# Inverse roots moved from ScalarE to VectorE, two loads moved later, and the queries' stacking DMAs issued by GpSimd, in a four-block transformer kernel

## The chip, the core and the metric

The kernel runs on one core of one Trainium2 chip. The core has five instruction streams: TensorE (PE, with its weight loads shown as PEld), VectorE (DVE), ScalarE (ACT), GpSimd (POOL) and SyncE (SP). They meet only at semaphores. The metric is the device time of one execution in microseconds (us). Batches, groups and units are counted from 0.

## The reference

For 8 batches of 512 tokens with 512 features the reference computes four residual blocks:

```python
x = x + attention(layernorm(x), ctx, ctx, Wq, bq, Wk, bk, Wv, bv, Wo, bo)   # 16 heads of 32
x = x + routed_experts(layernorm(x), Wc, bc, W1, b1, W2, b2)                # 32 experts, 4 sets, 32 wide
x = x + mlstm_heads(layernorm(x), ctx, ctx, igate, fgate)                   # 8 heads of 64, gated decay, RMS norm per head
x = x + bitlinear_ffn(layernorm(x), W1, b1, W2, b2)                         # 512 -> 2048 -> 512, 8-bit tokens, ternary weights

layernorm(x) = (x - mean) / sqrt(var + 1e-5)
rms(h)       = h * rsqrt(mean(h * h) + 1e-6)
```

All inputs and outputs are float32.

## The kernel before

Three phases follow each other, each a block of its own with the streams written out by hand: attention (`attention_phase`, names a_), experts (`experts_phase`, names b_) and the tail (`tail_phase`, names c_), which does the third and fourth block together. The experts' phase is not changed.

**Attention.** A batch has 64 units, one for each pair of a head and a tile of 128 queries. 16 units (4 heads by 4 tiles) form a group, so that a batch has the groups 0 to 3. The loop variable g runs over all units and some steps beyond the last; u is its place in the batch. In step g, PE does the score matmul of unit g+2 (`scores`, L604), the four transposes of the probabilities of unit g-1 (L612), every fourth step the mix with the values (L630), and one share of a product (K, Q, V, O or the router's L, after the list PRODUCTS; L680). DVE takes the maximum of a score tile (L491), ACT the exponential (L424), and the two take turns in copying the transposed probabilities out (L317).

The score matmul reads `stack["Q"]` and `stack["K"]`, in which each head's 32 rows stand four times, as high and low halves in two orders. The product of queries or keys for a group is split by ACT (high half, L415) and DVE (low half, `low`, L485) into `parts`; then 16 DMAs of 64 KB within SBUF (`stack_parts`, L309) write them into one of two stacks. The issuing queue first waits until the last score of the group two before has been done, and for DVE's low half. Before ACT writes `parts` for the next group, it waits until all 16 DMAs of the last one of the same kind have landed (`wait_stack` in `product_out`). ACT is in order: while it waits there, no exponential is made.

SP issues the 16 DMAs for the keys and then the 16 for the queries of a group (all but the first group's queries, which ACT issues), and in between the stores of the results. In each batch after the first, the splits fall in these steps: keys 1 in u=0, queries 1 in u=4, keys 2 in u=8, queries 2 in u=12, keys 3 in u=24, queries 3 in u=28; and keys 0 and queries 0 of the next batch in u=44 and 48. ACT issues the load of the next batch's x (`a_xs`) in u=4, of the residual x (`a_x`, L463) of the batch before in u=6, and of the context in u=33. POOL adds the output bias to the residual x, four adds (L368), and does nothing else.

The layernorm (class `Norm`) is spread over DVE's steps: statistics (L145), moments (L151), scale (L158), result (L162). In between, ACT takes the square root (`on_scalar`, L177). Its function is in another table than the exponential, so that ACT loads a table before and after it.

**Tail.** A Fori loop runs over the batches. Turn m does the mLSTM heads of batch m and the feed-forward block of batch m-1; at its end DVE runs one chain: moments and scale of the next batch's layernorm (`normalize_x2`), the heads' normalizer and RMS scale (L1597 to L1608), the products (L1610, L1618), the layernorm before the feed-forward (`on_vector`), and the 8-bit rounding of the tokens (L1623 to L1631, `c_xq`). PE begins the next turn with transposes of `c_xq` (L1651). There are three square roots on ACT in a turn.

Of the kernel before, what the change touches and what calls it, by code (L numbers as in the profile page):

```python
# [6 lines left out]
F32R = mybir.dt.float32r  # L7
ALU = mybir.AluOpType
# [3 lines left out]
P = 128  # L12
B, S, D = 8, 512, 512
T = S // P
# [115 lines left out]

class Norm:
# [3 lines left out]
    def __init__(self, ctx, sems, nc, name):  # L135
        self.nc = nc
        sb = lambda n, shape: ctx.enter_context(nc.sbuf_tensor(f"{name}_{n}", shape, F32))
        self.stats, self.mv, self.rstd = sb("stats", [P, T, 6]), sb("mv", [P, T, 2]), sb("rstd", [P, T])
        self.std = sb("std", [P, T])
        self.eps = sb("eps", [P, 1])  # L140
        self.var_ready = sems.make(f"{name}_var_ready")
        self.std_ready = sems.make(f"{name}_std_ready")
# [4 lines left out]
    def moments(self, dve, chain, last):  # L147
# [5 lines left out]
        dve.sem_inc(self.var_ready, 1)  # L153

    def scale(self, dve, chain, b):

        dve.wait_ge(self.std_ready, b + 1)
        chain.step(self.nc.vector.reciprocal(self.rstd[:, :], self.std[:, :]))  # L158
# [6 lines left out]
    def on_vector(self, dve, chain, b, src, dst):  # L165
# [4 lines left out]
        self.scale(dve, chain, b)  # L170
# [3 lines left out]

    def on_scalar(self, act, b):
        act.wait_ge(self.var_ready, b + 1)
        self.nc.scalar.activation(self.std[:, :], self.mv[:, :, 1], ACT.Sqrt,  # L177
                                  bias=self.eps[:, 0:1]).then_inc(self.std_ready, 1)


def attention_phase(nc, sems, A, scratch):
# [39 lines left out]
    STATS_AT, SCALE_AT, RESULT_AT = 14, 20, 21  # L221
# [25 lines left out]
    with ctx:  # L247
# [44 lines left out]
        filled, tie_ready, wq_ready, bo_ready, bo_full = (sem(n) for n in ("filled", "tie_ready", "wq_ready", "bo_ready", "bo_full"))  # L292
        sp_parted, pe_parted, act_parted = sem("sp_parted"), sem("pe_parted"), sem("act_parted")
        STACKED = 16 * 4 * HM
        N_LOADS = 6
# [16 lines left out]
        with nc.Block() as block:  # L312
# [8 lines left out]
            def _(sp):  # L321
                sp.dma_start(cs[:, :, :], tiled(A["ctx_1024"])[0]).then_inc(c_in, 16)
                sp.dma_start(w["Wk"][:, :, :], A["L0_xattn_Wk"].rearrange("(c p) n -> p c n", p=P)).then_inc(w_in["Wk"], 16)
                for name in ("Wv", "Wo"):
                    sp.dma_start(w[name][:, :, :], A["L0_xattn_" + name].rearrange("(c p) n -> p c n", p=P)).then_inc(w_in[name], 16)
# [30 lines left out]
            def _(pool):  # L356
                for ring in (work, score, turn, mix):
                    ring.give_ahead(pool)
                for norm in (norm0, norm1):
                    nc.gpsimd.memset(norm.eps[:, :], LN_EPS).then_inc(filled, 1)  # L360
# [3 lines left out]
                pool.wait_ge(bo_ready, 1)  # L364
                for b in range(B):
                    pool.wait_ge(x1_in, b * 16 + 16)
                    for t in range(T):
                        last = nc.gpsimd.tensor_tensor(x1[:, t, :], x1[:, t, :], bo[:, :], ALU.add)  # L368
                    last.then_inc(res_ready, 1)

            @block.scalar
            def _(act):
                act.dma_start(xs[:, :, :], tiled(A["x"])[0]).then_inc(x_in, 16)
                act.dma_start(w["Wq"][:, :, :], A["L0_xattn_Wq"].rearrange("(c p) n -> p c n", p=P)).then_inc(w_in["Wq"], 16)
                for name, tile in (("bq", bq), ("bk", bk), ("bv", bv)):
                    act.dma_start(tile[:, :], A["L0_xattn_" + name].rearrange("(c p) -> p c", p=P),
                                  allow_slow_non_contiguous=True).then_inc(loaded, 16)
# [3 lines left out]
                act.wait_ge(filled, 2)  # L381
# [47 lines left out]
                norm0.on_scalar(act, 0)  # L429
                act.wait_ge(loaded, 16 * N_LOADS)  # L430
                nc.scalar.mul(bq[:, :], bq[:, :], SCALE).then_inc(wq_ready, 1)
                act.wait_ge(w_in["Wq"], 16)
                nc.scalar.mul(w["Wq"][:, :, :], w["Wq"][:, :, :], SCALE).then_inc(wq_ready, 1)
# [5 lines left out]
                stack_parts(act, "Q", 0)  # L439
                act.dma_start(cs[:, :, :], tiled(A["ctx_1024"])[1]).then_inc(c_in, 16)  # L440
                for t in range(T):
                    product_out("V", 0, t)

                for g in range(STEPS):
# [10 lines left out]
                    if u == 4 and b + 1 < B:  # L455
                        act.wait_ge(xs_read, b + 1)
                        act.dma_start(xs[:, :, :], tiled(A["x"])[b + 1]).then_inc(x_in, 16)
                    if u == 6 and 1 <= b <= B:
                        if b >= 2:
                            act.wait_ge(x1_stored, (b - 1) * 16)  # L460
                            act.wait_ge(xn1_ready, b - 1)
# [4 lines left out]
                    if u == 33 and b + 2 < B:  # L466
                        act.dma_start(cs[:, :, :], tiled(A["ctx_1024"])[b + 2]).then_inc(c_in, 16)
                    if u == 39 and b >= 1:
                        norm1.on_scalar(act, b - 1)
# [5 lines left out]
            def _(dve):  # L475
# [59 lines left out]
                norm0.on_vector(dve, chain, 0, xs, xn).then_inc(xn_ready, 1)  # L535
# [4 lines left out]
                dve.wait_ge(bo_full, 1)  # L540
# [1290 lines left out]
```

## Time and profile before

| | us |
|---|---|
| median of 3 runs (2638.3 to 2654.33) | 2644.69 |
| the profiled execution, its own time | 2646.36 |
| its span, first to last instruction | 2644.6 |
| PE busy | 2224.4 (84%) |
| DVE busy | 1459.3 (55%) |
| ACT busy | 1411.9 (53%) |
| POOL busy | 365.0 (14%) |
| mean granted clock of TensorE | 0.906 |

The attention phase takes about the first 1190 us, the experts' phase the time to about 1580, the tail the rest. A busy share is the time in which an engine executes, over the span. In the timeline, the number in square brackets is the idle time of the engine ahead of a row, and behind the arrow stands what ended it. "SPq" and "ACTq" rows are DMA issues; their duration is that of the issue and not of the transfer.

### The profile page before, as it was taken

What the parts mean: (1) busy time and instruction counts of PE and PEld (TensorE: products, weight loads), DVE (VectorE), ACT (ScalarE), POOL (GpSimd) and SP (SyncE); (2) the same over time, 40 slices, a digit from 0 to 9 for tenths busy, and PEclk for the clock granted to TensorE, in tenths of its full rate; (3) what the DMA queues carried; (4) which work ended last, traced back from release to release, by engine and by line L of the source; (5) the groups of instructions that cost most, each with busy time, mean ns of one, the idle gap of its engine ahead of it and who ended that gap; (6) DMA issues with size and microseconds to landing.
All of it is one profiled execution on the core that took longest, in us unless ns stands there. A gap on an engine that the chain in (4) does not pass through costs nothing. (4 is left out here: it accounts for less than half of the span.)

```text
span 2644.6 us, 43219 instructions
## 1 busy us (share of the span) xinstructions
PE 2224.4 (84%) x14571; PEld 1402.8 (53%) x14571; DVE 1459.3 (55%) x2518; ACT 1411.9 (53%) x3038; POOL 365.0 (14%) x513
## 2 busy tenths in 40 slices
PE   6899999999999999876888854969888897979765
PEld 2565656565656565546647521646445454646442
DVE  1656566666665565642332322576766757566754
ACT  2665656565656565631332423766566574656553
POOL 0000000000000000002112100331313132231310
PEclk9999999999999999988998986779797888979787
DMA  4324343343333333316666667522212132132100
GB/s 151 97 77 116 87 104 112 97 120 97 112 97 105 94 91 87 96 56 167 176 229 175 192 220 249 196 96 69 87 59 93 57 121 89 62 99 68 34 15 16
DMA packets 200656, 288.78 MB, mean 109 GB/s; under 512 B 29408, under 2 KB 91904, under 8 KB 195264
## 3 DMA queue, kind: packets, MB, share of 16 engines
q1 hardware_dynamic: 157664, 232.86, 29.3%
q10 hardware_dynamic: 42848, 54.02, 6.8%
q8 instruction: 88, 1.44, 0.2%
q14 instruction: 56, 0.46, 0.1%
HBM read 156.62 MB, written 63.05 MB: 83 GB/s over the span
## 5 line engine op out<-in xcount | busy, mean ns | idle before, releaser
L491 DVE TENSOR_REDUCE a_negmax<-a_score 128x1 f32<-128x512 f32 x512 | 345.6, 684 | 120.4 <-PE a_score L604 110.5
L604 PE MATMUL a_score<-a_k_stack,a_q_stack 128*128 128x512 f32 x512 | 354.2, 692 | 67.4 <-ACT a_prob L424 67.4
L424 ACT ACTIVATE a_prob<-a_score,a_negmax 128x512 f32<-128x512 f32 x512 | 353.9, 694 | 57.0 <-DVE a_negmax L491 56.8
L612 PEld LDWEIGHTS a_turn<-a_ident,a_prob 128*128 128x128 f32 x2048 | 256.2, 142 | 132.3 <-issue 91.2
L317 ACT COPY a_probT<-a_turn 128x512 f32<-128x512 f32 x256 | 150.0, 586 | 325.4 <-PE a_turn L612 324.3
L612 PE MATMUL a_turn<-a_ident,a_prob 128*128 128x128 f32 x2048 | 311.9, 275 | 3.1 <-ACT a_perm L400 2.0
L317 DVE COPY a_probT<-a_turn 128x512 f32<-128x512 f32 x256 | 176.7, 690 | 244.4 <-PE a_turn L612 243.5
L1237 POOL TENSOR_SCALAR c_diag<-c_negm,c_aL 128x128 f32<-128x128 f32 x256 | 165.6, 664 | 342.7 <-issue 119.4
L1705 PE MATMUL c_work<-c_xT,c_cT 64*128 64x512 f32 (+3 forms) x512 | 179.2, 496 | 39.7 <-DVE c_decay L1473 39.7
L368 POOL TENSOR_TENSOR a_x<-a_x,a_bo 128x512 f32<-128x512 f32 x32 | 39.6, 1269 | 1122.5 <-DMA a_x<-in_x 1122.5
L604 PEld LDWEIGHTS a_score<-a_k_stack,a_q_stack 128*128 128x128 f32 x512 | 98.5, 192 | 175.3 <-ACT a_prob L424 89.0
L1705 PEld LDWEIGHTS c_work<-c_xT,c_cT 64*128 64x128 f32 x512 | 102.5, 210 | 136.0 <-issue 72.8
L1718 PE MATMUL c_mix<-c_v,c_decay 128*128 128x65 f32 x1280 | 174.0, 297 | 0.0
L1718 PEld LDWEIGHTS c_mix<-c_v,c_decay 128*128 128x128 f32 x1280 | 167.9, 212 | 4.7 <-issue 0.7
L1473 DVE SCALAR_TENSOR_TENSOR c_decay<-c_work,c_decay 128x512 f32<-128x512 f32 (+3 forms) x256 | 109.9, 483 | 91.2 <-PE c_work L1705 70.5
L869 PE MATMUL b_work<-b_blocks,b_xn 128*128 128x256 f32 x512 | 128.0, 415 | 26.3 <-POOL b_blocks L841 23.4
L1731 PE MATMUL c_ff<-c_w1T,c_xqT 128*128 128x512 bf16 x512 | 136.9, 429 | 11.3 <-ACT c_xqT L1262 11.3
L630 PE MATMUL a_mix<-a_probT,a_v 128*32 128x128 f32 x4096 | 145.7, 285 | 0.1
L1747 PE MATMUL c_ff<-c_w2T,c_hqT 128*128 128x512 bf16 x512 | 135.3, 424 | 10.6 <-ACT c_hqT L1278 10.6
L905 PE MATMUL b_work<-b_w2T,b_inner 128*128 128x512 f32 x256 | 126.5, 642 | 21.1 <-ACT b_inner L954 21.1
L1286 ACT ACTIVATE c_decay<-c_negm,c_aL 128x384 f32<-128x384 f32 (+2 forms) x192 | 83.5, 498 | 109.3 <-PE c_mix L1718 90.7
L869 PEld LDWEIGHTS b_work<-b_blocks,b_xn 128*128 128x128 f32 x512 | 123.4, 329 | 31.3 <-issue 24.1
(189 smaller groups left out, 3704.3 us busy)
## 6 DMA issues: line engine op xcount, KB each, us to landing
a_k_stack<-a_k_parts SPq DMA_DIRECT2D x512, 64.0 KB, 2.0
scratch_res<-b_res SPq DMA_DIRECT2D x32, 1024.0 KB, 4.7
c_res<-scratch_res SPq DMA_DIRECT2D x32, 1024.0 KB, 9.5
a_q_stack<-a_q_parts SPq DMA_DIRECT2D x496, 64.0 KB, 2.0
b_xn<-scratch_xn SPq DMA_DIRECT2D x68, 256.0 KB, 2.7
c_hid<-in_L_ffn_W ACTq DMA_DIRECT2D x16, 1024.0 KB, 5.2
c_negm<-scratch_m SPq DMA_DIRECT2D x64, 256.0 KB, 3.6
a_xs<-in_x ACTq DMA_DIRECT2D x8, 1024.0 KB, 6.8
```

What stands on the lines that cost most here:

```text
L317: copy(probT[:, U // HM % 2, U % HM, :, :], turn.bank(entries["P", U])[:, :].rearrange("p (k q) -> p k q", k=T)).then_inc(turn.free[entrie ...
L424: nc.scalar.activation(prob[:, U % 4, :], score.bank(U)[:, :], ACT.Exp, bias=negmax[:, u:u + 1], accum_out=sums[:, head_of(U), tile_of(U): ...
L491: nc.vector.tensor_reduce(negmax[:, U % UNITS:U % UNITS + 1], score.bank(U)[:, :], AX.X, ALU.max, negate=True).then_inc(max_ready, 1)
L604: nc.tensor.matmul(score.bank(U)[:, :], stack["Q"][:, M % 2, g, t * P:(t + 1) * P], stack["K"][:, M % 2, g, :], start=True, stop=True).the ...
L612: last = nc.tensor.transpose(turn.bank(j)[:, k * P:(k + 1) * P], prob[:, U % 4, k * P:(k + 1) * P], ident[:, :])
L630: last = nc.tensor.matmul(mix.bank(M)[g * DH0:(g + 1) * DH0, cols], v[:, b % 2, k, h * DH0:(h + 1) * DH0], probT[:, q % 2, g, k, :], start ...
L869: last = nc.tensor.matmul(work.bank(j)[:, c * EH * GT:(c + 1) * EH * GT], xc[:, 2 * half + c, :], blocks[:, t].rearrange("p e g -> p (e g) ...
L1237: last = nc.gpsimd.tensor_scalar(diag[:, h % 2, t, :], negm[:, h % 4, t * P:(t + 1) * P], aL[:, 0, t, h:h + 1], None, ALU.add)
L1705: last = nc.tensor.matmul(work.bank(j)[:, i0:i0 + S - t * P], cT[r, h // 2, t * P:(t + 1) * P], xT[r, h // 2, t * P:S], start=True, stop=True)
L1718: last = nc.tensor.matmul(mix.bank(job)[:, i * (DH1 + 1):(i + 1) * (DH1 + 1)], row_of(h, j, i * P, (i + 1) * P), head_of(v, h)[:, j], star ...
L1731: last = nc.tensor.matmul(ff.bank(j)[:, :], xqT[:, c, t * P:(t + 1) * P], w1T[:, c, k * 512:(k + 1) * 512], start=c == 0, stop=c == C - 1)
L1747: last = nc.tensor.matmul(ff.bank(j)[:, :], hqT[:, k, :], w2T[:, k, :], start=k == 0, stop=k == HC - 1)
```

## The change

- The square roots go. `inverse_root` computes 1/sqrt(value + eps) on DVE in 12 chained small steps: an integer shift and subtraction give a first guess, three Newton rounds of three steps refine it. Each step waits for the one before. It replaces ACT's root and DVE's reciprocal in all layernorms and in the RMS scale. In the attention loop its four parts stand in u=17 to 20 for the next batch's layernorm (statistics now in u=13 to 16), and in u=37 and 38 for the one before the experts.
- The load of x for the batch after the next is issued in u=26, the residual x in u=44 of its own batch, the context in u=43.
- SP issues the keys' stacking DMAs only. The queries' come from POOL's queue: groups 1, 2 and 3, then the wait for the residual x and the four adds, then group 0 of the next batch.
- At the start, Wk and Wq are loaded in two parts, the first 128 columns ahead; the last V product, the second K product and the bias product (L698) come after the first two scores, and the bias product inside the loop.

```diff
+def inverse_root(nc, step, dst, src, eps, value, square, parts=range(4)):
+    if 0 in parts:
+        step(nc.vector.tensor_scalar(value, src, eps, None, ALU.add))
+        step(nc.vector.tensor_scalar(dst.bitcast(I32), value.bitcast(I32), 1, None, ALU.logical_shift_right))
+        step(nc.vector.tensor_scalar(dst.bitcast(I32), dst.bitcast(I32), -1, 0x5F3759DF, ALU.mult, ALU.add))
+    for _ in [k for k in parts if k > 0]:
+        step(nc.vector.tensor_tensor(square, dst, dst, ALU.mult))
+        step(nc.vector.scalar_tensor_tensor(square, square, -0.5, value, ALU.mult, ALU.mult))
+        step(nc.vector.scalar_tensor_tensor(dst, square, 1.5, dst, ALU.add, ALU.mult))
...
 # SP
-                    stack_parts(sp, "Q", b * GROUPS + 1)
                     for m in (2, 3):
-                        for kind in ("K", "Q"):
-                            stack_parts(sp, kind, b * GROUPS + m)
+                        stack_parts(sp, "K", b * GROUPS + m)
...
                     if b + 1 < B:
-                        for kind in ("K", "Q"):
-                            stack_parts(sp, kind, (b + 1) * GROUPS)
+                        stack_parts(sp, "K", (b + 1) * GROUPS)
 # POOL
-                pool.wait_ge(bo_ready, 1)
+                stack_parts(pool, "Q", 0)
                 for b in range(B):
+                    for m in (1, 2, 3):
+                        stack_parts(pool, "Q", b * GROUPS + m)
+                    pool.wait_ge(bo_ready, 1)
                     pool.wait_ge(x1_in, b * 16 + 16)
                     for t in range(T):
                         last = nc.gpsimd.tensor_tensor(x1[:, t, :], x1[:, t, :], bo[:, :], ALU.add)
                     last.then_inc(res_ready, 1)
+                    if b + 1 < B:
+                        stack_parts(pool, "Q", (b + 1) * GROUPS)
 # ACT, in the loop over g
-                    if u == 4 and b + 1 < B:
-                        act.dma_start(xs[:, :, :], tiled(A["x"])[b + 1]).then_inc(x_in, 16)
-                    if u == 6 and 1 <= b <= B:
-                        act.dma_start(x1[:, :, :], tiled(A["x"])[b - 1]).then_inc(x1_in, 16)
-                    if u == STATS_AT + T + 1 and b + 1 < B:
-                        norm0.on_scalar(act, b + 1)
-                    if u == 39 and b >= 1:
-                        norm1.on_scalar(act, b - 1)
+                    if u == 26 and b + 2 < B:
+                        act.dma_start(xs[:, :, :], tiled(A["x"])[b + 2]).then_inc(x_in, 16)
+                    if u == 44 and b < B:
+                        act.dma_start(x1[:, :, :], tiled(A["x"])[b]).then_inc(x1_in, 16)
 # DVE, tail
-                    dve.wait_ge(rms_ready, m + 1)
-                    step(nc.vector.reciprocal(f3[:, :, :], f2[:, :, :]))
+                    inverse_root(nc, step, f3[:, :, :], f2[:, :, :], 1e-6, f4[:, :, :], f5[:, :, :])
```

## Rows read from the trace of the kernel before

**Rows 1.** Busy time in a stretch: length, then PE, PEld, DVE, ACT, POOL, clock, DMA.
```profile
204.00:344.00 140.00, 131.64 (x1041) 84.28 (x1040) 86.37 (x150) 84.36 (x195) 4.94 (x4) 0.99 0.38 103
```
**Rows 2.** Waits from 60 to 1153 us: total, times, longest.
```profile
PE a_score L604 <- ACT a_prob L424: 67.4, 30, 4.8
...
ACT a_k_parts L415 <- DMA a_k_stack<-a_k_parts: 35.2, 8, 6.0
ACT a_q_parts L415 <- DMA a_q_stack<-a_q_parts: 6.4, 2, 3.8
```
**Rows 3.** Timeline around the stall of batch 2: start, duration, engine, line, operation.
```profile
330.25 10.01 SPq L309 DMA_DIRECT2D a_k_stack<-a_k_parts  x16
337.17 0.74 DVE L485 SCALAR_TENSOR_TENSOR a_q_parts<-a_work,a_bq,a_q_parts 128x512 fp32r<-128x512 f32 x1
337.40 0.38 ACTq L463 DMA_DIRECT2D a_x<-in_x  x1
340.36 10.63 SPq L309 DMA_DIRECT2D a_q_stack<-a_q_parts  x16
347.36 0.69 ACT L415 ACTIVATE a_k_parts<-a_work,a_bk 128x512 fp32r<-128x512 f32 x1 [4.92 <-DMA a_k_stack<-a_k_parts]
348.76 0.67 PE L604 MATMUL a_score<-a_k_stack,a_q_stack 128*128 128x512 f32 x1 [3.71 <-ACT a_prob L424]
350.21 1.93 PE L630 MATMUL a_mix<-a_probT,a_v 128*32 128x128 f32 x32
355.19 0.69 ACT L415 ACTIVATE a_q_parts<-a_work,a_bq 128x512 fp32r<-128x512 f32 x1
```
**Rows 4.** Busy time just behind that stall; the clock is the last but two.
```profile
350.00:352.00 2.00, 2.00 (x34) 1.36 (x32) 1.29 (x2) 0.54 (x2) 2.00 (x2) 0.50 0.42 110
```
**Rows 5.** Lines of ACT, 60 to 1150 us: busy, mean ns, idle.
```profile
L177 ACT ACT_TABLE_LOAD x14 | 18.0, 1283 | 0.3
```
**Rows 6.** Timeline: PE behind a square root in batches 0, 1 and 7.
```profile
107.26 0.50 PE L604 MATMUL a_score<-a_k_stack,a_q_stack 128*128 128x512 f32 x1 [2.38 <-ACT a_prob L424]
...
276.24 0.50 PE L604 MATMUL a_score<-a_k_stack,a_q_stack 128*128 128x512 f32 x1 [1.55 <-ACT a_prob L424]
...
1112.66 0.50 PE L604 MATMUL a_score<-a_k_stack,a_q_stack 128*128 128x512 f32 x1 [3.71 <-ACT a_prob L424]
```
**Rows 7.** Line L309, issues: ns least, median, most; and time to landing.
```profile
L309 SPq DMA_DIRECT2D a_k_stack<-a_k_parts x512: 507/591/2077, 27.8 to 1097.7; - x171
...
DMA to landing us min/median/max: 1.9/2.0/8.7
```
**Rows 8.** Timeline: ACT's stacking issues at the start.
```profile
34.74 10.57 ACTq L309 DMA_DIRECT2D a_q_stack<-a_q_parts  x16
```
**Rows 9.** Line L604: ns least, median, most; first and last start.
```profile
L604 PE MATMUL a_score<-a_k_stack,a_q_stack x512: 398/795/1240, 63.8 to 1148.5; 128*128 128x512 f32 x171
```
**Rows 10.** Timeline at the end of the attention phase.
```profile
1165.20 7.13 PE L680 MATMUL a_work<-a_Wo,a_attnT 128*128 128x512 f32 x16 [2.00 <-DVE a_x L516]
```
**Rows 11.** Timeline of one tail turn's chain on DVE, and PE behind it.
```profile
2080.33 0.38 DVE L151 BATCH_NORM_AGGREGATE c_norm_mv<-c_norm_stats 128x2 f32<-128x6 f32 x4 [0.33 <-DVEq L104]
2081.43 1.91 DVE L162 TENSOR_SCALAR c_xn<-c_x,c_norm_mv,c_norm_rstd 128x512 f32<-128x512 f32 x4
...
2084.75 0.19 DVE L1605 TENSOR_TENSOR c_f<-c_f 128x32 f32<-128x32 f32 x1
...
2085.72 0.19 DVE L1608 TENSOR_TENSOR c_f<-c_f 128x32 f32<-128x32 f32 x1
...
2104.91 1.89 PE L1651 MATMUL c_ff<-c_identb,c_xq 128*128 128x128 bf16 x16 [6.61 <-DVE c_xq L1631]
```
**Rows 12.** Timeline of the same turn: small DVE steps beside POOL's adds.
```profile
2096.98 4.93 POOL L1248 TENSOR_TENSOR c_x<-c_x,c_b 128x512 f32<-128x512 f32 x4 [40.30 <-DVEq L1622]
...
2099.53 0.18 DVE L1625 RECIPROCAL c_xr<-c_xscale 128x4 f32<-128x4 f32 x1
2099.74 0.97 DVE L1626 TENSOR_SCALAR c_xr<-c_xr 128x4 f32<-128x4 f32 x1
```

More of the change, by code:

```diff
@@ L7 @@
 F32R = mybir.dt.float32r
+I32 = mybir.dt.int32
 ALU = mybir.AluOpType
@@ L152, in moments, with scale @@
         chain.step(last, apart=True)
[L153 to L158, printed above, removed]
+    def scale(self, chain, parts=range(4)):
+        inverse_root(self.nc, chain.step, self.rstd[:, :], self.mv[:, :, 1], LN_EPS, self.value[:, :], self.square[:, :], parts)
     def tile_result(self, src, dst, t):
@@ L163, in tile_result, with on_vector @@
                                             ALU.subtract, ALU.mult)
-    def on_vector(self, dve, chain, b, src, dst):
+    def on_vector(self, dve, chain, src, dst):
         for t in range(T):
@@ L169, in on_vector @@
         self.moments(dve, chain, last)
-        self.scale(dve, chain, b)
+        self.scale(chain)
         for t in range(T):
@@ L173, in on_vector @@
         return last
[L175 to L178, printed above, removed]
 def attention_phase(nc, sems, A, scratch):
@@ L534, in _ @@
                 dve.wait_ge(x_in, 16)
-                norm0.on_vector(dve, chain, 0, xs, xn).then_inc(xn_ready, 1)
+                norm0.on_vector(dve, chain, xs, xn).then_inc(xn_ready, 1)
                 dve.wait_ge(xn_ready, 1)
@@ L539, in _ @@
                 low("Q", 0, 0)
-                dve.wait_ge(bo_full, 1)
-                nc.vector.tensor_tensor(bo[:, :], bo[:, :], mix.bank(0)[:, :], ALU.add).then_inc(bo_ready, 1)
                 maximum(0)
@@ L553, in _ @@
                                 low(*job)
+                    if g == 3:
+                        dve.wait_ge(bo_full, 1)
+                        nc.vector.tensor_tensor(bo[:, :], bo[:, :], mix.bank(0)[:, :], ALU.add).then_inc(bo_ready, 1)
                     if g % UG == 0 and UG <= g <= ALL:
@@ L570, in _ @@
                             norm0.moments(dve, chain, last)
-                        if u == SCALE_AT:
-                            norm0.scale(dve, chain, b + 1)
+                        if SCALE_AT <= u < SCALE_AT + 4:
+                            norm0.scale(chain, (u - SCALE_AT,))
                         if RESULT_AT <= u < RESULT_AT + T:
@@ L579, in _ @@
                     if b >= 1:
+                        if u in (37, 38):
+                            norm1.scale(chain, (2 * (u - 37), 2 * (u - 37) + 1))
                         if u == 39:
-                            norm1.scale(dve, chain, b - 1)
                             if b >= 2:
@@ L692, in _ @@
                 pe.wait_ge(w_in["Wv"], 16)
-                for t in range(T):
+                for t in range(T - 1):
                     product("V", 0, t, range(C))
-                pe.wait_ge(w_in["Wo"], 16)
-                pe.wait_ge(loaded, 16 * N_LOADS)
-                for c in range(C):
-                    last = nc.tensor.matmul(mix.bank(0)[:, :], bv[:, c:c + 1].to_broadcast([P, P]), w["Wo"][:, c, :],
-                                            start=c == 0, stop=c == C - 1)
-                last.then_inc(bo_full, 1)
-                pe.wait_ge(bo_ready, 1)
-                product("K", 0, 1, range(C))
                 for U in range(AHEAD):
                     scores(U)
+                product("V", 0, T - 1, range(C))
+                pe.wait_ge(w_in["Wk"], 16)
+                product("K", 0, 1, range(C))
+                pe.wait_ge(wq_ready, 3)
                 for g in range(STEPS):
@@ L717, in _ @@
                         turn_tiles(*job)
+                    if g == 1:
+                        pe.wait_ge(w_in["Wo"], 16)
+                        pe.wait_ge(loaded, 16 * N_LOADS)
+                        pe.sem_inc(pe_parted, 1)
+                        for c in range(C):
+                            last = nc.tensor.matmul(mix.bank(0)[:, :], bv[:, c:c + 1].to_broadcast([P, P]), w["Wo"][:, c, :],
+                                                    start=c == 0, stop=c == C - 1)
+                        last.then_inc(bo_full, 1)
 def experts_phase(nc, sems, A, scratch):
@@ L1037, in tail_phase @@
         b1, b2 = sb("b1", [P, HID]), sb("b2", [P, D])
-        one, eps6 = sb("one", [P, 1]), sb("eps6", [P, 1])
+        one = sb("one", [P, 1])
         rnd = sb("rnd", [P, 1])
@@ L1055, in tail_phase @@
         hraw = sb("hraw", [P, T, PAIRS, 2 * DH1 + 2])
-        f1, f2, f3 = (sb(f"f{k}", [P, T, H1]) for k in range(3))
+        f1, f2, f3, f4, f5 = (sb(f"f{k}", [P, T, H1]) for k in range(5))
         square, sumsq = sb("square", [P, T, DH1]), sb("sumsq", [P, T, H1])
@@ L1404, in turn @@
                                 load_weight(PIECES + h + 1)
-                        if next_too and h == H1:
-                            norm0.on_scalar(act, m + 1)
-                    if m is not None:
-                        act.wait_ge(meansq_ready, m + 1)
-                        nc.scalar.activation(f2[:, :, :], f2[:, :, :], ACT.Sqrt, bias=eps6[:, :]).then_inc(rms_ready, 1)
                     if next_too:
@@ L1509, in normalize_x2 @@
                     norm0.moments(dve, chain, last)
-                    norm0.scale(dve, chain, m)
+                    norm0.scale(chain)
                     for t in range(T):
@@ L1619, in turn @@
                     step(last)
-                    step(norm1.on_vector(dve, chain, m, x3, x2))
+                    step(norm1.on_vector(dve, chain, x3, x2))
                     dve.sem_inc(x3_read, 1)
```

80 lines of the change are left out of this document (40 added, 40 removed).

## Prediction

> **What bounds the kernel now.** I read the busy time by stage first. In a full batch of the attention phase PE is busy 131.64 of 140 us and DVE and ACT about 86 each [rows 1]: PE sets the pace, and only its gaps of some 8 us a batch can be won there. The list of waits says what the gaps are: nearly all of them, 67.4 us, are score matmuls that wait for an exponential [rows 2]. ACT's own waits show the cause of over half: 35.2 us for the keys' stacking DMAs and 6.4 us for the queries', in ten waits [rows 2]. The timeline shows one. ACT comes to the split of keys 2 at 347.36 - 4.92 = 342.44 us, the DMAs of keys 1 were issued from 330.25 to 340.26, and yet they land 5 us late, behind a 1 MB load issued at 337.40 (and one of the same size two units ahead of it); PE idles 3.71 us of the 4.92 [rows 3]. Behind it the granted clock is 0.50, that is 1.2 GHz instead of 2.4 [rows 4], and a mix takes 1.93 us [rows 3]; with some 2.9 us at half clock such a stall costs 1.4 us more. The rest of the gaps stands behind table loads: 14 loads of the root's table at 1.28 us [rows 5], each followed by one back to the exponential's, with PE idle 2.38 us behind the next batch's layernorm, 1.55 us behind the other, and 3.71 us in batch 7, where no products fill the steps [rows 6].
>
> The tail is bound otherwise. At a turn's end PE waits 6.61 us for `c_xq`, the last link of DVE's chain [rows 11]. What makes that chain longer makes the turn longer.
>
> **The change part by part.** All of it is set against the profiled execution, 2646.36 us with a span of 2644.6; the median of the runs is 1.7 us below it.
>
> *Loads moved.* With x issued in u=26, the residual in u=44 and the context in u=43, no 1 MB load runs beside the stacking of keys 1. SP ends its issues at 340.26, and with 2.0 us from an issue to its landing [rows 7] the last lands at about 341.6, ahead of ACT's 342.44 [rows 3]. The ten waits go, if nothing takes their place. PE loses about 1.2 us less than ACT in each (3.71 against 4.92), so 41.6 - 9 x 1.2 = 31 us. Seven of them are about as long as the one shown, and I give them its lower clock too: 7 x 1.4 = 10 us. Together -41. The moved loads collide with the stacking of keys 0 and queries 0 of the next batch, which is needed some 16 units later: nothing.
>
> *Roots in the attention loop.* ACT loses both loads and the root. PE gets back 7 x 2.38 + 6 x 1.55 + 3.71 and 1.4 for the clock in batch 7 [rows 6]: -31. DVE gets 12 steps for each. A small step starts 0.21 us after the last one (2099.53 to 2099.74) [rows 12]. DVE idles (140 - 86.37) / 64 = 0.84 us in a unit [rows 1], so three steps (0.63) in each of u=17 to 20 fit, and six (1.26) in u=37 and 38 are 0.4 too many each: 7 x 0.8, and a little more in batch 7, whose units are short: +7 (0 to 15).
>
> *The queries' DMAs on POOL.* SP issues less, which frees nothing that PE waits for once the loads have gone, except that queries 1 no longer wait for SP to end keys 1 (340.36 against DVE's end at 337.91) [rows 3]. What counts is when they land. ACT needs all 16 to be down when it comes to the split of queries 2. In the run before it comes there 7.83 us after that of keys 2 (347.36 to 355.19), 1.4 of it due to the low clock [rows 3]; without the stall it comes at 342.44 + 6.4 = 348.8, which is 10.9 us after DVE's low half of queries 1. If POOL needs r us for an issue, the last lands 16 r + 1.4 us after it, 1.4 being the landing's 2.0 less one issue. ACT waits 16 r - 9.5, and PE 1.2 us less; where PE's stall is as long as the one shown, 1.4 for the clock comes on top. Behind ACT's wait stand the exponentials, and so PE. The trace has no DMA issued by POOL. The nearest rows are the same 16 transfers on SP (10.01 / 16 = 0.63 us each) and on ACT (10.57 / 16 = 0.66) [rows 3, 8]; a single one takes up to 2.08 [rows 7]. Below it is bounded by 0.51, the shortest issue. I take r = 1.0: nearer to the many than to the one, but above them, since both rows are of the other two queues and it would be chance if POOL's way of making a transfer cost the same. Then ACT waits 6.5 us, PE 5.3 + 1.4 = 6.7, in eight batches +53 us; +52, since queries 1 of batch 0 have a little more room. At r = 0.63 it is 0.6 us, within the slack, and nothing; at 1.3, 11.3 - 1.2 + 1.4 = 11.5 us or +92; at 2.08 POOL would issue for 133 us of a batch and set its pace, beyond +180. The other groups have room at r = 1.0: queries 2, 3 and 0 take 18 us and have 15 units or more, about 31 us, except group 0, which stands behind the residual's load and adds and has about 23.
>
> The Trainium skill (DMA: Bandwidth & Descriptors, "Latency and other measured facts") gives about 1 us to the first byte for a DMA issued by GpSimd and 0.6 us for one from the other queues. If the difference of 0.4 lies in each issue, r is 0.63 + 0.4 = 1.03, and the sum is mine; if it lies only once in the way of each transfer, r stays 0.63 and the sum is the first rival's. No row of this trace says which.
>
> *The start.* ACT no longer issues 16 DMAs (34.74 to 45.31) [rows 8], so the V copies are made at once; the first score, now at 63.8 [rows 9], goes ahead of two products but waits for POOL's 16: 34.74 + 16 + 1.4 = 52 us. Two scores, two products (3.5 us each) and the bias product in the loop follow, and the two added load issues of 0.5 us each stand ahead of ACT's first copy: +2 (-4 at r = 0.63, +7 at 1.3).
>
> *The last batch.* Its residual is there early, which saves the 2.00 us of PE's wait [rows 10]; its last root is on the path and costs 1.8 more. Nothing.
>
> *Roots in the tail.* A layernorm's scale takes 2081.43 - 2080.71 = 0.72 us from the end of the moments to the first result [rows 11], since ACT has loaded its table ahead. Twelve steps at 0.21 are 2.52: +1.80. The RMS root takes 2085.72 - 2084.75 = 0.97 us with the step ahead of it [rows 11]; after, 13 x 0.22 = 2.86: +1.89. A turn gets +5.5, all in the chain that PE waits 6.61 us for; PE's own transposes in between are later by 1.8 only, and are hidden. Eight turns: +44; I take +41, since the first turn has its root behind other work of ACT's (36 to 48). What ACT saves in the tail hides behind the same wait.
>
> Sum: -41 - 31 + 7 + 52 + 2 + 41 = +30 on 2646.4: **2676 us**.
>
> **The rivals.**
>
> *POOL issues as fast as SP.* For it: the transfers are the same 64 KB, and the small POOL instructions are not slow. Against it: no row has such an issue. Then the +52 goes, and the start gives 4 where it took 2, rounded to -3: -41 - 31 + 7 - 3 + 41 = -27, 2619 us. This is the case on the other side. It decides between r = 0.75 and 0.85: at 0.85 ACT waits 4.1 us and PE 2.9, 23 us over eight batches, and the sum is near nothing.
>
> *POOL issues at 1.3 us or more.* Then +92 stands for +52, the start costs 6 or 7, and queries 0 (16 x 1.3 + 1.4 = 22 us behind the adds, against some 23) begin to hold up the next batch's scores, about 1 us each, +8: -72 + 7 + 92 + 7 + 8 + 41 = +83, about 2728 us.
>
> *The added steps on DVE are slowed by POOL.* Such a thing has a row: beside POOL's four adds a 128x4 tensor_scalar takes 0.97 us where the reciprocal ahead of it takes 0.18 [rows 12]. If POOL's making of descriptors acts as its adds do, the three such steps of u=17, which now stand beside the issues for queries 2, cost 2.4 us more, less the slack 0.8: 7 x 1.6 = +11, 2687 us. The Trainium skill (SBUF — State Buffer, "Who interferes with whom") says that DVE's two-port modes and GpSimd lock each other out, and that descriptors made by GpSimd wait for such an operation. The trace agrees for the adds, by the 0.97; for descriptors nothing here shows it.
>
> **How the numbers follow.** I give 0.37 to the forecast (r of 0.85 to 1.15, own range 2646 to 2702), 0.33 to the first rival, 0.25 to the second, 0.05 to the third alone. The range of 8 in 10 goes from just under the first rival to just over the second: 2614 to 2734. This kernel's runs can tell a change of about 0.5%, 13 us. Slower by more than that come out the second and third rivals (0.29 of 0.30) and most of the forecast's case (0.28 of 0.37): 0.57. Faster is the first rival but for its upper edge, and a sliver of the others: 0.30. The same: 0.13.
>
> **What would show it.** A POOL queue row `a_q_stack` with 16 issues in about 16 us; ACT's waits for the keys' DMAs gone and one of about 6 us a batch for the queries' in u=12; no root tables on ACT; DVE's time from the moments to `c_xn` at 2.5 us in place of 0.72, and PE's wait for `c_xq` near 10 us with the turn 5.5 us longer. The forecast is wrong if POOL's 16 issues take 12 us or less, or over 20, or if the root's step isn't near 0.21 us.

## The result, and the profile after

The changed kernel takes 2615.56 us (median of 4 runs, 2610.33 to 2623.96) against 2645.79 us for the kernel before beside it: a ratio of 0.9893, interval 0.9866 to 0.9919. The forecast was 2676 us and slower; the kernel is 30 us faster. The profiled execution took 2620.14 us with a span of 2618.4.

By stages of the profiled executions (attention ends where PE starts `b_aux`, the tail starts with PE's first `c_mix`):

| stage | before | after | difference |
|---|---|---|---|
| start and attention phase | 1199.39 | 1115.32 | -84.1 |
| experts phase (same code) | 390.2 | 385.3 | -4.9 |
| tail | 1055.0 | 1117.8 | +62.8 |

The attention phase brought more than forecast and the tail cost more. The experts' code is the same in every kernel here and took 384 to 396 us in the profiled executions, so its -4.9 says nothing. First the page of the changed kernel: the busy times, the queues, and time from issue to landing.

```profile
PE 2216.2 (85%) x14571; PEld 1398.9 (53%) x14571; DVE 1524.9 (58%) x2958; ACT 1347.6 (51%) x2952; POOL 616.1 (24%) x1020
...
q0 software_dynamic: 16384, 33.59, 5.0%
q8 instruction: 88, 1.44, 0.2%
q14 instruction: 89, 0.73, 0.1%
...
a_k_stack<-a_k_parts SPq DMA_DIRECT2D x512, 64.0 KB, 2.7
a_q_stack<-a_q_parts POOLq DMA_DIRECT2D x512, 64.0 KB, 2.3
```

The answer to [rows 1] is the busy time of a stretch of 128 us in batches 2 and 3. A middle batch, from its first score to the next batch's, now takes 130.7 us where it took 139.5 to 143. PE idles 0.8 us of the stretch, and its clock is full (1.00, that is 2.4 GHz).

```profile
322.00:450.00 128.00, 127.23 (x1026) 81.38 (x1025) 88.17 (x170) 78.14 (x187) 36.17 (x68) 1.00 0.39 112
```

The answer to [rows 2], the waits of the attention phase (total, times, longest): PE's 67.4 us behind exponentials are 7.6, ACT's 35.2 and 6.4 us for stacks are 4.0 and 0.7.

```profile
PE a_score L614 <- ACT a_prob L434: 7.6, 10, 2.3
ACT a_k_parts L425 <- DMA a_k_stack<-a_k_parts: 4.0, 7, 0.7
ACT a_q_parts L425 <- DMA a_q_stack<-a_q_parts: 0.7, 1, 0.7
```

The row that the forecast hung on, from the timeline of POOL (start, duration): 16 issues in 7.81 us, that is 0.49 us each, where SP took 0.63 [rows 3]. The third rival, that POOL's issues slow DVE's added steps, falls with the same trace: the 128x4 steps of the roots take 0.16 to 0.18 us in the attention phase, as long as in the run below that has the roots on DVE and no issue on POOL.

```profile
324.79 7.81 POOL L316 DMA_DIRECT2D a_q_stack<-a_q_parts  x16 [6.25 <-DVE a_q_parts L493]
```

In the tail the answers to [rows 11] are a timeline of one turn on DVE and PE. From the last aggregate to the layernorm's first result it is now 2.71 us (2161.29 to 2164.00). PE waits 10.86 us for `c_xq`, 4.3 more than before. Two rows have no forerunner: DVE starts the next turn 3.19 us after its last instruction, "issue" being the cause, and PE then waits 2.49 us for the hidden layer.

```profile
2160.91 0.38 DVE L164 BATCH_NORM_AGGREGATE c_norm_mv<-c_norm_stats 128x2 f32<-128x6 f32 x4 [0.15 <-DVEq L105]
2161.44 0.17 DVE L138 TENSOR_SCALAR c_norm_value<-c_norm_mv 128x4 f32<-128x4 f32 x1 [0.15 <-DVEq L105]
...
2164.00 1.92 DVE L173 TENSOR_SCALAR c_x<-c_x,c_norm_mv,c_norm_rstd 128x512 f32<-128x512 f32 x4 [0.21 <-DVE c_norm_rstd L144]
...
2174.05 1.89 PE L1657 MATMUL c_ff<-c_identb,c_xq 128*128 128x128 bf16 x16 [10.86 <-DVE c_xq L1637]
2177.11 0.74 DVE L1531 TENSOR_SCALAR c_gate_rows<-c_work,c_gb 8x512 f32<-8x512 f32 x1 [3.19 <-issue]
...
2183.82 1.89 PE L1737 MATMUL c_ff<-c_w1T,c_xqT 128*128 128x512 bf16 x4 [2.49 <-DVE c_hid L1438]
```

In the kernel before the same instruction came 0.70 us after `c_xq`:

```profile
2105.47 0.74 DVE L1524 TENSOR_SCALAR c_gate_rows<-c_work,c_gb 8x512 f32<-8x512 f32 x1 [0.70 <-DVE c_xq L1631]
```

The stall stands at the head of the five turns that DVE's loop jumps back to (3.19 to 3.54 us). The turn that enters the loop and the one behind it have 0.42 and 0.39. And the DMA view of one turn of the changed kernel (1918.4 to 2048 us) has a line that no middle turn of the kernel before has, instruction packets (their number, MB, share):

```profile
q14 instruction: 5, 0.04, 0.1%
```

### The profile page after: what moved, and what is told of

Its sections match the earlier page's. It is cut to its first block and busy times, and to the rows that moved or that the text cites. A ratio compares the mean times of both kernels' runs of the same rounds, so it can differ in the third digit from the quotient of the medians.

```text
span 2618.4 us, 43758 instructions
## 1 busy us (share of the span) xinstructions
PE 2216.2 (85%) x14571; PEld 1398.9 (53%) x14571; DVE 1524.9 (58%) x2958; ACT 1347.6 (51%) x2952; POOL 616.1 (24%) x1020
## 5 line engine op out<-in xcount | busy, mean ns | idle before, releaser
L316 POOL DMA_DIRECT2D a_q_stack<-a_q_parts x512 | 250.8, 498 | 513.1 <-DVE a_q_parts L493 253.8
L1711 PE MATMUL c_work<-c_xT,c_cT 64*128 64x512 f32 (+3 forms) x512 | 185.2, 510 | 39.7 <-DVE c_decay L1480 39.7
L1737 PE MATMUL c_ff<-c_w1T,c_xqT 128*128 128x512 bf16 x512 | 142.3, 439 | 18.7 <-ACT c_xqT L1278 10.5
L643 PE MATMUL a_mix<-a_probT,a_v 128*32 128x128 f32 x4096 | 138.4, 276 | 0.1
```

The source lines that it names most:

```text
L316: eng.dma_start(stack[kind][i * DH0:(i + 1) * DH0, M % 2, g, :].bitcast(F32), parts[kind][g * DH0:(g + 1) * DH0, part, :].bitcast(F32)).th ...
L1711: last = nc.tensor.matmul(work.bank(j)[:, i0:i0 + S - t * P], cT[r, h // 2, t * P:(t + 1) * P], xT[r, h // 2, t * P:S], start=True, stop=True)
L1737: last = nc.tensor.matmul(ff.bank(j)[:, :], xqT[:, c, t * P:(t + 1) * P], w1T[:, c, k * 512:(k + 1) * 512], start=c == 0, stop=c == C - 1)
```

## The experiments

Two theories were at stake. In the attention phase: POOL's queue costs nothing at 0.49 us an issue, and the loads, the queries' queue and the roots each bring a part; which part brings what was open. In the tail: the roots' chain is only half the loss, and the other half is DVE's loop, whose longer code is fetched again in every turn. The kernel before was measured again beside each of three groups of the twelve kernels; its medians were 2644.47, 2647.38 and 2649.64 us, and a difference of some 5 us between groups is scatter.

**The tail's roots back on ACT** (the faster kernel of the two halves)

```
 tail_phase: as in the kernel before (ACT Sqrt, reciprocal on DVE); attention_phase: as changed
```

> The changed kernel with the tail's three roots a turn back on ACT, as before (attention phase and start as changed). Theory: the tail lost 63 us (1055.0 to 1117.8 from the first mix on PE to the end) through its roots on DVE and nothing else, so this kernel takes 2616 - 63 = 2553 us, with a turn back at 119.5 us and DVE starting a turn 0.7 us after c_xq. Rival 1: part of the loss came from outside (the clock's history or other phases): then only the 44 us of my own chain price come back, 2572 us. Rival 2: the attention phase's gain of 84 us depends on nothing in the tail; if it shrank here, the phases would not add up and the time would be above 2580.

2564.64 us, ratio 0.9692 (0.9653 to 0.973). The tail is back at 1056.7 us, the turns are 119.4 us, DVE starts them after 0.70. So the whole of the tail's loss is undone, which the first rival denied, and the attention phase's gain stays (1116.77), which the second did. The total is 12 us above the theory's figure: 61 us went from the tail, but the profiled run of the changed kernel, from whose 62.8 the figure was made, was 4.6 us above its median, and the experts phase took 3.4 us more here.

**Only the tail's roots on DVE**

```
 tail_phase: as changed; attention_phase: as in the kernel before
```

> The mirror image: the kernel before with only the tail's roots moved to DVE. Theory: before + 63 = 2708 us, turns of 126 to 130 us, DVE starting a turn of the loop over 3 us after c_xq with instruction packets in each turn. Rival: the price in my prediction, +41 to +44, 2687 to 2690 us.

2723.65 us, ratio 1.029 (1.025 to 1.033): +79, more than either. The tail takes 1137.4 us, 82 more than before. The same loop body, yet DVE's stall is 5.3 to 5.6 us, and the hidden layer waits 4.8:

```profile
2157.86 0.74 DVE L1570 TENSOR_SCALAR c_gate_rows<-c_work,c_gb 8x512 f32<-8x512 f32 x1 [5.52 <-issue]
...
2164.58 1.89 PE L1776 MATMUL c_ff<-c_w1T,c_xqT 128*128 128x512 bf16 x4 [4.81 <-DVE c_hid L1477]
```

So the stall depends on more than the body. The code ahead of the loop differs; whether the loop's place among the fetched blocks decides was not tried.

**The changed kernel with DVE's turns written out**

```
+            if eng is nc.vector:
+                for b in range(B - 2):
+                    turn(b + 1, b, True)
+            else:
                 with eng.Fori(0, B - 2) as b:
                     turn(b + 1, b, True)
```

> The changed kernel with DVE's six middle turns of the tail written out instead of in a loop (the other engines keep theirs). Theory: DVE's loop body of 345 instructions in the built program (282 before) no longer fits what the engine holds, so that each turn of the loop starts with a stall of 3.2 us and instruction packets; written out, the instructions come ahead of need, the stall of five turns goes and with it the later hidden layer and its low clock: 5 turns of 129.5 become 125 us or less, 2616 - 22 = 2594 us or lower. Rival 1: the stall is the branch itself or the wait for another engine's loop: the same 3.2 us stay, 2616. Rival 2: the added turn length is the longer chain alone and the stall is hidden: the stall goes but the time falls under 5 us.

2594.57 us, ratio 0.9799 (0.9769 to 0.9829): 21 us off, as the theory said (in the profiled executions the tail alone is 32 us shorter, 1085.7 for 1117.8, so the loop's price is 20 to 30 us). In place of the stall stand 0.23 us:

```profile
2164.34 0.74 DVE L1535 TENSOR_SCALAR c_gate_rows<-c_work,c_gb 8x512 f32<-8x512 f32 x1 [0.23 <-DVE c_xq L1641]
```

Both rivals fall. The turns are 123.0 to 124.8 us for the first run's 119.4, so the chain alone costs some 4 us a turn.

**The first run with 64 increments in DVE's loop**

```
                         if m is not None and h < H1:
                             head_product(m, h)
+                        if 1 <= h:
+                            for _ in range(8):
+                                dve.sem_inc(dve_parted, 1)
```

> The kernel of the first run (roots of the tail on ACT, DVE's loop body 282 instructions, no stall at its start) with 64 semaphore increments added to DVE's loop of the tail, eight behind each head's product, where DVE has time; they bring its body to 346 instructions and lengthen no chain of data. Theory: the stall at the loop's start is a matter of the number of instructions, so it appears here at 3 to 5.5 us in five turns with instruction packets in each, and the turn grows by 2 to 5 us: 2565 + 10 to 25 = 2580 us. Rival: the stall needs the root's instructions (their register operations or the chain); then none appears and the time stays at 2565, or gains a few us by the increments' own time.

2586.63 us, ratio 0.9768 (0.9741 to 0.9795): 22 us above the first run. No root is on DVE's path here, and the stall and its packets (five in the turn from 2034 us on) appear, first the timeline, then the DMA view:

```profile
2159.93 0.74 DVE L1591 TENSOR_SCALAR c_gate_rows<-c_work,c_gb 8x512 f32<-8x512 f32 x1 [3.19 <-issue]
```

```profile
q14 instruction: 5, 0.04, 0.1%
```

The turns that end in the stall are 121.1 to 123.4 us long, where the first run has 118.6 to 119.5. The one turn of the loop without a stall at its end is 120.1 for 119.2, so the increments' own time is 1 us at most. With the run before it, this shows that a loop longer by 63 or 64 instructions brings the stall, whatever they compute. That count alone sets it is not shown: the run with only the tail's roots on DVE has the same count and a longer stall.

**The first run with DVE's turns written out** (the edit of the last run but one)

> The kernel of the first run (2565 us) with DVE's six middle turns of the tail written out. Its loop has no stall, only 0.70 us between c_xq and the next turn's first instruction, which becomes 0.23. Theory: nothing to win but that: 5 x 0.5 = 2.5 us, 2562. Rival: the register instructions that prepare a loop's wait values (81 of 282) cost time on the chain to c_xq, and the written-out form, which waits on constants, brings 10 us or more, 2555; the run of the changed kernel written out had turns of 123.3 us where the chain's price in the prediction, 5.5, would have given 125.

2561.49 us, ratio 0.9655 (0.962 to 0.969), 3 us below the first run, which is within the scatter. The rival falls: in the changed kernel a 128x4 step of a root starts 0.20 us after the last in the loop and 0.20 written out, so the register instructions cost nothing there. Against the changed kernel written out, this one gives the chain's price alone: 2594.57 - 2561.49 = 33 us by the medians. The tail's stage says less, 1085.7 - 1062.2 = 24 us against this run and 29 against the first, so the chain costs about 30.

**Queries back on SP** (otherwise the first run)

```
                         stack_parts(sp, "K", b * GROUPS + 1)
-                    for m in (2, 3):
-                        stack_parts(sp, "K", b * GROUPS + m)
+                    stack_parts(sp, "Q", b * GROUPS + 1)
+                    for m in (2, 3):
+                        for kind in ("K", "Q"):
+                            stack_parts(sp, kind, b * GROUPS + m)
```

> The kernel of the first run (tail as before, attention phase as changed) with all queries' stacking DMAs back on SP's queue behind the keys' of the same group. Theory: queries 1 start 2.4 us later, when SP has ended keys 1, at 0.6 us an issue; ACT then waits about 2.3 us for them at the split of queries 2 and PE about 1.1 in each of 8 batches, some 9 us, and the first score comes some 5 us later: 2553 + 14 = 2567 us. Rival 1: POOL's queue is what brought the 21 us by which the attention phase beat my other terms: 2574 us or more. Rival 2: it is worth nothing, 2553 us.

2591.41 us, ratio 0.98 (0.9764 to 0.9836), 27 us above the first run; the attention phase ends at 1143.73, also 27 later, 5 of it a first score at 48.42 in place of 43.47. The first rival holds. ACT waits for the queries in eight batches, 2.9 us each, and PE 24.1 us for exponentials where it waited 7.7 in the first run:

```profile
ACT a_q_parts L474 <- DMA a_q_stack<-a_q_parts: 23.4, 8, 4.1
```

**Only the loads moved**

```
-                    if u == 4 and b + 1 < B:     (x, b + 1)
-                    if u == 6 and 1 <= b <= B:   (residual, b - 1)
-                    if u == 33 and b + 2 < B:    (context)
+                    if u == 26 and b + 2 < B:    (x, b + 2)
+                    if u == 43 and b + 2 < B:    (context)
+                    if u == 44 and b < B:        (residual, b)
```

> The kernel before with only the loads moved (x at u=26 two batches ahead, the residual at u=44 of its own batch, the context at u=43). Theory: -41 as in the prediction, 2605 us, ACT's waits for the keys' stack gone, and with them most of PE's 3.7 us stalls. Rival 1: something takes the place of the keys' waits (the queries' DMAs on the same queue, the table loads), gain of 15 to 25, about 2625 us. Rival 2: the loads bring more than priced, since the low clock behind a stall goes too: -55 to -60, 2588 us.

2632.0 us, ratio 0.9942 (0.9922 to 0.9962), -12. The first rival holds in its cause, the queries' DMAs on the same queue; its 15 to 25 us overlap what the interval allows (10 to 21). The waits for the keys are gone, and others stand in their place, eight of them where there were two:

```profile
ACT a_q_parts L415 <- DMA a_q_stack<-a_q_parts: 27.3, 8, 4.1
ACT a_k_parts L415 <- DMA a_k_stack<-a_k_parts: 1.5, 5, 0.5
```

One of them in the timeline: SP issues the queries' DMAs only when it has ended the keys', up to 352.34 us, and ACT stands from 350.55 on.

```profile
331.03 11.17 SPq L309 DMA_DIRECT2D a_k_stack<-a_k_parts  x16
342.30 10.04 SPq L309 DMA_DIRECT2D a_q_stack<-a_q_parts  x16
353.82 0.69 ACT L415 ACTIVATE a_q_parts<-a_work,a_bq 128x512 fp32r<-128x512 f32 x1 [3.27 <-DMA a_q_stack<-a_q_parts]
```

The title says that two loads are moved later. In fact three move, and only the context's is issued later (u=43 for u=33 of the same batch). The next x is issued 42 units earlier than before, the residual 26.

**Only the queries on POOL**

```
-                    stack_parts(sp, "Q", ...)           (all groups)
-                stack_parts(act, "Q", 0)
+                stack_parts(pool, "Q", 0)               (ahead of POOL's loop)
+                        stack_parts(pool, "Q", b * GROUPS + 1)      (then the adds for b - 1, then 2, 3 and 4)
```

> The kernel before with only the queries' stacking DMAs moved to POOL (the first group's too, ahead of the loop; POOL's adds for a batch stand behind the next batch's queries 1, where its late residual load puts them). Theory: the 1 MB loads still stand beside the keys' DMAs, so the keys' waits stay; only the 6 us of waits for queries go and ACT's V copies at the start come earlier: 2637 us. Rival: POOL's queue brings its 20 to 27 us here as well, 2620 us.

2646.34 us, ratio 0.9995 (0.9968 to 1.0021): -3, which is nothing within the scatter. The first score comes at 54.33 instead of 63.75, but the keys' waits have grown from 35.2 to

```profile
ACT a_k_parts L421 <- DMA a_k_stack<-a_k_parts: 45.8, 8, 7.1
```

**Loads moved and queries on POOL**

```
 both edits above; POOL: queries 1, 2, 3 of the batch, its adds, queries 0 of the next
```

> The kernel before with the loads moved and the queries' DMAs on POOL; the roots stay on ACT and the start keeps its order but for the first group. Theory: the two parts need each other. Loads alone gave 10 to 12 us, because ACT then waited 27 us for the queries behind the keys on SP; together they give the 41 us of the prediction's term for the loads: 2604 us. Rival: they add up without help from one another, 12 for the loads and what the run with the queries alone gives (8 or so): 2625 us.

2599.01 us, ratio 0.9807 (0.9777 to 0.9836): -51, where the parts alone give -12 and -3. They need each other. The phase ends at 1144.58, 54.8 earlier, 9.7 of it at the first score (54.10); in the loop the pair brings 45 us. What is left of the waits:

```profile
ACT a_k_parts L417 <- DMA a_k_stack<-a_k_parts: 5.3, 6, 1.9
ACT a_q_parts L417 <- DMA a_q_stack<-a_q_parts: 0.7, 1, 0.7
```

**Only the attention phase's roots on DVE**

```
-                    if u == STATS_AT + T + 1 and b + 1 < B:
-                        norm0.on_scalar(act, b + 1)
-                    if u == 39 and b >= 1:
-                        norm1.on_scalar(act, b - 1)
+                        if SCALE_AT <= u < SCALE_AT + 4:
+                            norm0.scale(chain, (u - SCALE_AT,))
+                        if u in (37, 38):
+                            norm1.scale(chain, (2 * (u - 37), 2 * (u - 37) + 1))
```

> The kernel before with only the attention phase's roots moved to DVE (12 small steps each, at the changed kernel's places). The prediction's terms: -31 + 7 = -24, 2621 us. Rival 1: the roots bring more, since the PE gaps beside the table loads also bring the low clock: -35 to -45, 2605 us. Rival 2: they bring less, since the waits for the keys' DMAs, which stay, grow by what ACT gains: -10, 2635 us.

2623.77 us, ratio 0.9899 (0.9871 to 0.9927): -23.6 for -24. The attention phase ends 28.9 earlier. ACT's waits for the keys stay as they were (36.5 us for 35.2), so the second rival falls, and the interval (19 to 34) ends below the first.

**POOL slowed, first size** (128x480 fills)

```
                                   ...).then_inc(stack_in[kind][M % 2], 16)
+                    if kind == "Q":
+                        padded.append(0)
+                        nc.gpsimd.memset(pad[:, :], 0.0).then_inc(pad_done, 1)
+                        eng.wait_ge(pad_done, len(padded))
```

> The kernel of the first run (tail as before, attention as changed; 2565 us) with a 128x480 fill of half a microsecond behind each of the queries' DMAs on POOL, so that an issue takes about 1.0 us there, the value that the prediction took. The prediction's price: 52 us in eight batches and 9 us for a later first score, of which some is hidden: 2565 + 52 + 9 = 2626 us, and in each batch a wait of ACT of about 6.5 us at the split of queries 2. Rival 1: only the price was wrong and also the path: the queries' stack is not needed so early, ACT waits under 2 us, 2575 us. Rival 2: the fills themselves slow DVE's work beside them; then DVE's small steps of u=17 would be longer and the time above 2640.

2682.33 us, ratio 1.0131 (1.0103 to 1.0159). I had missed the aim: the issues are 1.30 us apart, since 0.29 us stand between a fill and the next issue. ACT's waits are 10.4 us each for the formula's 11.3, so the first rival falls. The second has its sign: the time is above 2640, and one of the small steps beside the fills takes 0.45 us in the mean for 0.18. But all that DVE's slowed instructions lose is under 15 us of the 118. POOL's timeline, and ACT's row in the list of waits:

```profile
320.18 0.50 POOL L367 DMA_DIRECT2D a_q_stack<-a_q_parts  x1 [0.29 <-POOL a_pad L371]
320.67 0.52 POOL L371 MEMSET a_pad<- 128x480 f32 x1
321.48 0.50 POOL L367 DMA_DIRECT2D a_q_stack<-a_q_parts  x1 [0.29 <-POOL a_pad L371]
```

```profile
ACT a_q_parts L480 <- DMA a_q_stack<-a_q_parts: 83.0, 8, 12.9
```

**POOL slowed, second size** (`pad` 120 columns wide)

> As the run with fills behind the queries' DMAs on POOL, whose issues came out 1.30 us apart (0.50 the DMA, 0.52 the fill, 0.29 between them) and not 1.0; with a fill of 120 columns in place of 480 (0.2 us) they should now be 1.0 us apart, the value of the prediction. There ACT waited 83.0 us in eight waits, 10.4 each, where the prediction's formula 16 r - 9.5 gives 11.3. Theory: the formula holds with an offset of 10.4, so 5.6 us a wait here and 2565 + 8 x (5.6 - 1.2 + 1.4) + 9 = 2620 us; read in proportion to the other run (118 us for 10.4) it is 2628. Rival: the cost is in the fills beside DVE and not in the late landing; then it falls with their busy time from 118 to about 45 us, 2610, while ACT's wait stays near 10.

2631.32 us, ratio 0.9922 (0.9898 to 0.9947): 67 us above the first run. Issues are 1.00 us apart (333.23 to 334.23), and ACT waits 5.9 us a batch in the mean, where the formula gives 6.5. The fills' busy time fell from 265 to 111 us and ACT's wait with the issue time, and the small steps on DVE take their 0.16 to 0.18 us again, so the rival falls. The same two views:

```profile
333.23 0.50 POOL L367 DMA_DIRECT2D a_q_stack<-a_q_parts  x1 [22.61 <-PE a_score L669]
333.72 0.22 POOL L371 MEMSET a_pad<- 128x120 f32 x1
334.23 0.50 POOL L367 DMA_DIRECT2D a_q_stack<-a_q_parts  x1 [0.29 <-POOL a_pad L371]
```

```profile
ACT a_q_parts L480 <- DMA a_q_stack<-a_q_parts: 47.1, 8, 8.4
```

## Why the prediction was wrong

**The failed step is r, the time of one issue on POOL.** I took 1.0 us, above the rows of SP and ACT, "since both rows are of the other two queues and it would be chance if POOL's way of making a transfer cost the same", and bounded it below by 0.51. It is 0.49 to 0.50, under that bound, which was SP's shortest issue and no bound for POOL. With it the +52 is 0 and the forecast turns into the first rival, 2619 us, to which I gave 0.33; the time is 2616. That they agree so well is luck: the attention phase gained 84 us where the rival's terms give 68, and the tail lost 63 where they give 41, and the two errors nearly cancel.

The rest of the step was right. With issues made 1.00 us apart, ACT waited 5.9 us for the 6.5 of 16 r - 9.5, and the attention phase ended 64.4 us later (1181.20 against 1116.77), 7.5 of them at the first score: 57 us in the loop for the forecast's 52. At 1.30 the wait was 10.4 for 11.3, and the kernel 118 us slower in all. So the way from an issue's time to the kernel's was sound, and its input was a guess: no row of before showed an issue on POOL.

The Trainium skill (DMA: Bandwidth & Descriptors, "Latency and other measured facts") puts POOL's first byte 0.4 us later than the other queues', about 1 us against 0.6. Read as a price of each issue, that would give the 1.03 of the prediction. The runs show it in no issue, and from issue to landing they show no such difference either: POOL's transfers land after 2.3 us and SP's after 2.7 in the changed kernel, where both queues are busy together, and where POOL's issues stand 1.00 us apart its transfers land after 1.9, for 2.0 on SP when SP issues all. When the first byte moves, no view here shows.

**Loads moved, -41.** The size held, the account did not. I wrote that SP's shorter queue "frees nothing that PE waits for once the loads have gone". The run with the loads alone refutes it: -12, with 27.3 us of new waits for queries that stand behind the keys on SP. Their late start was priced (2.4 us), but in the term of POOL's queue and not as a condition of this one. The rows held the wait: on SP the last of queries 1 lands at 340.36 + 10.63 + 1.4 = 352.4 us [rows 3], and I had ACT there at 348.8, which is 3.6 us a batch; 3.4 were measured. The 41 belongs to the pair, which brings 45 in the loop.

**Roots in the attention loop, -31 + 7.** Measured alone -23.6 by the medians and -28.9 in the stage; on top of the pair the phase ends 27.8 us earlier (1144.58 to 1116.77), the rest of the start included. The sum was right; there PE's waits for exponentials fall by 29 us (36.6 to 7.7), so that the +7 for DVE hardly shows.

**The start, +2** (-3 in the rival). The first score comes at 42.81, not at 52. Of that gain, 9.7 us are the first group's DMAs no longer on ACT. The further 11 us pay for two products and the bias product that now stand behind it, as forecast: the roots with this order bring 27.8 us, and without it 28.9. About -10.

**Roots in the tail, +41.** The added steps have the size I gave them (0.20 us for 128x4, 0.22 for 128x32), and the chain's price, taken between the two kernels that are written out, is 33 us by the medians and 24 by the tails. What was missing is another term, the loop, which I put at nothing without a word: 21 us by writing it out, 22 us by the increments alone. In the built program DVE's body grew from 282 to 345 instructions. The engine then stands 3.2 to 3.5 us at each jump back, five instruction packets pass in each turn (two in a written-out one, without a stall), and the hidden layer's first products are late. The mean granted clock of a turn is 0.83 to 0.85 where it is 0.87 in the first run, but the loop is not all of that: with the increments alone it is 0.86, and with the roots written out 0.83 to 0.89. The Trainium skill has the rule (Runtime: NRT & Kernel Launch, "Instruction fetch mechanics"): an engine holds only a few blocks of code, and a jump back whose target has left them stalls until it is fetched. The runs agree in kind: no stall with 282 instructions of the built program, a stall with 345 and 346. A count between them was not tried, nor the same count at another place in the code. I had not weighed that rule.

Laid end to end, the runs split the change: in the stages, loop of the attention phase -45 - 28, start -10, experts phase -5, tail +63, together -25 for the -26 between the two profiled executions; by the medians -80 for the attention phase (the first run), +33 for the chain, +21 for the loop, less the 3 that writing out gives anyway, together -29. Each term is the difference of two neighbouring runs, so such sums close by themselves and are no test. Of what the forecast said would show it wrong, the first sign came: POOL's 16 issues took less than 12 us.

The best kernel is then the changed attention phase with the roots of the tail on ACT: 2564.64 us, or 2561.49 with DVE's turns written out, 3% below the kernel before.

## What to carry to other kernels

Where a forecast hangs on a price that no row shows, look for how little it could cost as hard as for how much; a row of another queue is no bound. Two queues' waits that end within a few us of each other have to be lifted together: alone the two edits brought 12 us and 3, together 51. Small instructions in an engine's loop cost their duration, and once the loop is long enough a stall at every jump back: where a loop starts its turns with an idle "issue" and instruction packets in the DMA view, shorten the body, move work to an engine with room, or write the loop out.

## What the runs showed of the hardware that was not expected

- A 64 KB DMA between SBUF tiles is issued in 0.50 us on POOL (median of 512), less than the 0.59 on SP [rows 7]. In the changed kernel it lands after 2.3 us on POOL and 2.7 on SP; after 1.9 on POOL with its issues 1.00 us apart, and after 2.0 on SP when SP issues all.
- From the last instruction of one turn to the first of the next DVE stands 0.7 us with 282 instructions in its loop and 3.2 to 3.5 us with 345 (the changed kernel) or 346 (the increments); in the kernel with only the tail's roots on DVE, also 345, it is 5.3 to 5.6 us, for which no run gives the cause. Written out it is 0.23 us.
- On POOL 0.29 us pass between a fill that raises a semaphore and the next instruction that waits for it.
- In DVE's loop the register instructions that prepare the waits take no time that shows: root steps start 0.20 us apart with them and without.
